# Moving two weight-update products ahead of the first mixture, and multiplying the last two down units of both mixtures unsplit

## The reference

```python
x = x + tanh(g_xattn[0]) * L0_xattn(layernorm(x), ctx, mask)   # stage 0: 16 heads of 8
x = x + tanh(g_ffn[0])   * L0_ffn(layernorm(x))                # stage 1: mixture, 16 experts, top 4
x = x + tanh(g_xattn[1]) * L1_xattn(layernorm(x), ctx, ctx)    # stage 2
x = x + tanh(g_ffn[1])   * L1_ffn(layernorm(x))                # stage 3: fake-quantised weights + LoRA
x = x + tanh(g_xattn[2]) * L2_xattn(ctx, layernorm(x))         # stage 4
x = x + tanh(g_ffn[2])   * L2_ffn(layernorm(x))                # stage 5: 8 experts, top 2
x = x + tanh(g_xattn[3]) * L3_xattn(layernorm(x), ctx, ctx)    # stage 6: 16 heads of 8
x = x + tanh(g_ffn[3])   * L3_ffn(layernorm(x))                # stage 7: mixture, 64 experts, top 6
```

```python
h = silu(einsum('th,eih->tei', x, gate_w)) * einsum('th,eih->tei', x, up_w)
routed = einsum('te,teh->th', combine, einsum('tei,ehi->teh', h, down_w))
base = einsum('bsi,oi->bso', x, fake_quant(W)) + b       # twice in L1_ffn
lora = einsum('bsr,or->bso', einsum('bsi,ri->bsr', x, A), B)   # rank 16
return base + 2 * lora
```

## Time and profile before

| | us |
|---|---|
| median of 3 runs | 596.26 |
| lowest, highest | 595.03, 597.34 |
| the profiled execution's own time | 596.09 |
| its span in the trace | 594.3 |
| busy: PE, PEld | 564.9, 409.6 |
| busy: DVE, ACT, POOL | 381.7, 387.9, 245.7 |

### The profile page before, as it was taken

How to read it: one execution, slowest core, us unless ns; L and a number is a source line. 1 busy time by engine, 2 the same in 40 slices (tenths; PEclk the granted TensorE clock), 3 DMA queues, 4 the chain that set the end, 5 groups by cost and what they waited for, 6 DMA issues and landing times.

```text
span 594.3 us, 10734 instructions
## 1 busy us (share of the span) xinstructions
PE 564.9 (95%) x3703; PEld 409.6 (69%) x3703; DVE 381.7 (64%) x736; ACT 387.9 (65%) x787; POOL 245.7 (41%) x231
## 2 busy tenths in 40 slices
PE   9999998999999997999899999999989999999997
PEld 6567766687665775776555556577768788888885
DVE  2678857556641657777354676478838666666665
ACT  4277877655666447888665656677875576666663
POOL 5006683486013100111015781000023788888884
PEclk9999999999999999999999999999999999999999
DMA  8300001161000000000000102000001666665740
GB/s 258 139 2 2 2 1 33 28 159 54 0 2 1 1 0 1 1 2 1 2 0 3 39 15 66 1 2 1 3 9 36 165 176 169 181 184 169 192 123 36
DMA packets 14852, 33.55 MB, mean 56 GB/s; under 512 B 2913, under 2 KB 8433, under 8 KB 14673
## 3 DMA queue, kind: packets, MB, share of 16 engines
q1 hardware_dynamic: 14800, 32.89, 19.4%
HBM read 32.03 MB, written 0.85 MB: 55 GB/s over the span
## 4 chain that ended last, share of the span: by engine, by line
PE 73%; DVE 9%; ACT 7%; issue 7%; POOL 3%; ACTq 0%; DVEq 0%; POOLq 0%
PE bank L842 9%; PE bank L844 8%; PE bank L843 8%; PE bank L726 5%; PE bank L737 4%; PE bank L752 3%; PE bank L685 3%; ACT wa L1408 2%; PE bank L700 2%; PE bank L648 2%; PE bank L1243 2%; PE bank L642 2%; PE bank L1118 2%; PE bank L1132 2%; PE bank L1107 1%
## 5 line engine op out<-in xcount | busy, mean ns | idle before, releaser
L502 POOL TENSOR_TENSOR h_lo<-wc,h_hi 128x512 fp32r<-128x512 f32 x56 | 72.6, 1300 | 15.2 <-ACT h_hi L1477 15.2
L842 PE MATMUL bank<-xn_hi,w_hi 128*128 128x512 f32 x168 | 66.0, 393 | 3.4 <-DVE xn_lo L1962 3.1
L844 PE MATMUL bank<-xn_hi,w_lo 128*128 128x512 f32 x168 | 65.4, 390 | 0.0
L843 PE MATMUL bank<-xn_lo,w_hi 128*128 128x512 f32 x168 | 65.4, 389 | 0.0
L1951 DVE TENSOR_TENSOR wb<-arena,bank 128x512 f32<-128x512 f32 x64 | 44.0, 687 | 32.9 <-PE bank L844 32.8
L1477 ACT ACTIVATE h_hi<-wc 128x512 fp32r<-128x512 f32 x56 | 35.3, 633 | 39.4 <-DVE wc L1959 29.8
L494 POOL TENSOR_TENSOR w_lo<-ring,w_hi 128x384 fp32r<-128x384 f32 x42 | 42.7, 1019 | 17.7 <-ACT w_hi L1454 17.7
L1739 DVE TENSOR_TENSOR wa<-bank,row_max 128x512 f32<-128x512 f32 x64 | 44.3, 692 | 7.5 <-ACT wb L1354 4.3
L1354 ACT ACTIVATE wb<-wa 128x512 f32<-128x512 f32 x64 | 40.1, 630 | 13.7 <-DVE wa L1739 13.3
L1735 DVE TENSOR_REDUCE row_max<-bank 128x4 f32<-128x512 f32 x64 | 43.6, 682 | 5.9 <-PE bank L726 5.4
L502 POOL TENSOR_TENSOR h_lo<-arena,h_hi 128x512 fp32r<-128x512 f32 x26 | 33.7, 1295 | 24.2 <-ACT h_hi L1477 24.2
(11 more groups left out here) (347 smaller groups left out, 1393.0 us busy)
## 6 DMA issues: line engine op xcount, KB each, us to landing
arena<-comb_rows SPq DMA_DIRECT2D x64, 256.0 KB, 4.1
ring<-in_experts SPq DMA_DIRECT2D x42, 192.0 KB, 2.5
ring<-in_experts SPq DMA_DIRECT2D x8, 256.0 KB, 3.2
mats<-in_mats SPq DMA_DIRECT2D x1, 1472.0 KB, 10.2
mats<-in_mats SPq DMA_DIRECT2D x1, 832.0 KB, 6.7
mats<-in_mats SPq DMA_DIRECT2D x2, 320.0 KB, 7.9
x<-in_x_t SPq DMA_DIRECT2D x1, 512.0 KB, 4.3
context<-in_ctx_t SPq DMA_DIRECT2D x1, 512.0 KB, 4.9
```

Source lines behind the costliest of these rows:

```text
L502: nc.gpsimd.tensor_tensor(h_lo[:, v % 3, :], hidden_of(v), h_hi[:, v % 3, :].bitcast(f32), ALU.subtract).then_inc(m_h_lo, 1)
L842: mm(out, w, x_, start=start, stop=False)
L843: mm(out, w, x_rest, start=False, stop=False)
L844: return mm(out, w_rest, x_, start=False, stop=stop)
```

## The change

Three things are done.

1. **The two weight updates** leave stage 1's mixture and take the place of the first two `keep_warm` calls in the drain of `attn(0)`; they write banks 3 and 2. VectorE instead of ScalarE copies them to `wd`: the first copy ahead of the last `divide`, the second behind it. The remaining idle products of the drain go to bank 1. In the mixture `combine_t` now waits for the evacuation of the values (`b_vev`) alone, and the norm's variance products wait for `d_up_out` first.
2. **The last two down products** of each mixture take the hidden activation and the ring's weights as they are, in one fp32 product each, instead of three fp32r products. The rounding on ScalarE and the rests on POOL and VectorE of these two units are gone. The counts of `m_h_hi` and `m_h_lo` are lower by two for each mixture, so the waits on them in the second subtract 2.
3. **The load of ring slot 3** for stage 5 waits until all down products of the first mixture are done, since the last pair's weights are now read from the ring itself.

```diff
@@ SP
             for e in range(4):
+                if e == 3:
+                    sp.wait_ge(m_down, MOE[0]["units"])
                 sp.dma_start(ring[:, e, 0:384], a["experts2"][e]).then_inc(w_in[e], 16)
@@ POOL, moe
-                    pool.wait_ge(m_h_hi, u0 + v + 1)
+                    pool.wait_ge(m_h_hi, u0 - 2 * n + v + 1)
...
-                for v in range(2, m["units"] - 1):
+                for v in range(2, m["units"] - 2):
                     hidden_rest(v)
@@ TensorE, attn
                 probs_v(B - 1, 3)
-                keep_warm(2, bank[3])
+                if inst == 0:
+
+                    pe.wait_ge(in_mats1, 32)
+                    mm(bank[3][:, :], lora[:, 0:P], lora[:, P:5 * P], start=True, stop=True).then_inc(d_lora, 1)
+                else:
+                    keep_warm(2, bank[3])
                 tail(B - 1, 1)
-                keep_warm(3, bank[3])
+                if inst == 0:
+                    for j in range(4):
+                        last = mm(bank[2][:, j * P:j * P + P], lora[:, 5 * P + j * P:5 * P + j * P + P],
+                                  lora[:, 9 * P:10 * P], start=True, stop=True)
+                    last.then_inc(d_lora, 1)
+                else:
+                    keep_warm(3, bank[3])
                 tail(B - 1, 2)
-                keep_warm(2, bank[3])
+                keep_warm(2, bank[1])
                 tail(B - 1, 3)
-                keep_warm(2, bank[3])
+                keep_warm(2, bank[1])
@@ TensorE, moe
                     c, slot = v % 2, slot_of(v // 2)
-                    pe.wait_ge(m_h_lo, u0 + v + 1)
+                    if v >= m["units"] - 2:
+
+                        pe.wait_ge(m_h, u0 + v + 1)
+                        mm(bank[6 + c][:, :], ring[:, slot, 256:384], hidden_of(v), start=False, stop=True)\
+                            .then_inc(m_down, 1)
+                        return
+                    pe.wait_ge(m_h_lo, u0 - 2 * n + v + 1)
...
                 for v in range(4, 6):
                     gate_up(v)
-                    if n == 0:
-                        updates1(v - 4)
                 if n == 0:
                     for half in range(2):
-                        pe.wait_ge(d_up_out, half + 1)
+                        pe.wait_ge(b_vev, half + 1)
@@ TensorE, program
             attn(0)
-            norm(NORM_OF[1][0], 2)
+            norm_means(NORM_OF[1][0])
+            keep_warm(2, bank[4])
+            pe.wait_ge(d_up_out, 2)
+            norm_rest(NORM_OF[1][0])
             moe(MOE[0])
@@ ACT, moe
-                if n == 0:
-                    for c in range(2):
-                        act.wait_ge(d_lora, c + 1)
-                        fn(wd[:, c, :], bank[2 + 3 * c][:, :], ACT.Copy).then_inc(d_up_out, 1)
...
                 for v in range(2, m["units"]):
-                    hidden(v)
+                    if v < m["units"] - 2:
+                        hidden(v)
@@ DVE, attn
                 units(base, extra)
+                if inst == 0:
+                    dve.wait_ge(d_lora, 1)
+                    v.tensor_copy(wd[:, 0, :], bank[3][:, :]).then_inc(d_up_out, 1)
                 divide(B - 1)
+                if inst == 0:
+                    dve.wait_ge(d_lora, 2)
+                    v.tensor_copy(wd[:, 1, :], bank[2][:, :]).then_inc(d_up_out, 1)
@@ DVE, moe (the same in far_gated)
                     if unit >= 3:
-                        dve.wait_ge(m_h_lo, u0 + unit - 2)
+                        dve.wait_ge(m_h_lo, u0 - 2 * n + unit - 2)
...
-                unit = m["units"] - 1
-                dve.wait_ge(m_h_hi, u0 + unit + 1)
-                dve.wait_ge(m_down, u0 + unit - 2)
-                dve.wait_ge(m_h_lo, u0 + unit)
-                v.tensor_tensor(h_lo[:, unit % 3, :], hidden_of(unit), h_hi[:, unit % 3, :].bitcast(f32),
-                                ALU.subtract).then_inc(m_h_lo, 1)
                 for c in range(2):
```

More of the change, by code:

```diff
@@ L819, in values1 @@
                     last.then_inc(b_v, 1)
[L821 to L829, removed]
             def moe(m):
@@ L864, in down @@
                     c, slot = v % 2, slot_of(v // 2)
-                    pe.wait_ge(m_h_lo, u0 + v + 1)
+                    if v >= m["units"] - 2:
[4 more added lines that the diff above has]
+                    pe.wait_ge(m_h_lo, u0 - 2 * n + v + 1)
                     product(bank[6 + c][:, :], w_hi[:, slot, 256:384], w_lo[:, slot, 256:384],
-                            h_hi[:, v % 3, :], h_lo[:, v % 3, :], v < 2, v >= m["units"] - 2).then_inc(m_down, 1)
+                            h_hi[:, v % 3, :], h_lo[:, v % 3, :], v < 2, False).then_inc(m_down, 1)
                 def weight(v):
```

## The result

The changed kernel takes 594.19 us, the median of 11 runs from 592.21 to 595.83; the kernel before, run beside it 11 times, takes 597.25 (595.03 to 599.18). The ratio is 0.9948, 95% interval 0.9935 to 0.9962: 3.1 us faster. The forecast was a gain of 4.42 and 591.8 us, and its range ended at 594.0. The prediction was wrong: the median lies 0.2 us above its range, and the gain is 1.4 us short. The profiled execution took 595.83, with a span of 594.0.

What follows compares the result with a forecast made beforehand. TensorE, at full clock and busy most of the span, was taken as the bound. -3.29 - 0.84 - 0.84 + 0.55 = -4.42 us gave 591.8 us expected, range 590.0 to 594.0.

Steps and rivals of the forecast that it cites:

- Part 1: First mixture without the two updates: the transposes of the combine weights and all behind them come earlier, -3.29 us.
- that rival: First mixture: the gain from removing the updates is not handed on, hardly any of it left, 595.1 us; chance 0.06.
- its half: First mixture: half the updates' gain kept back, 593.5 us; chance 0.15, shared with one more low-clock stretch.
- Part 2: Ends of both mixtures: unsplit last down products let the last addition start earlier, -0.84 us each.
- Part 3: Drain of the first attention: the moved updates delay transposes, reciprocal and the norm's variance products, +0.55 us.
- most of what stands there are full products: Drain of the first attention: argument, beside hardly more idle time, against the clock falling to 1.2 GHz there.
- the drain goes cold: Rival: clock falls to 1.2 GHz in the drain and stays down through norm, router and first units, 597.4 us or more; chance 0.04.
- the first rival: Low clock at other joints or nowhere: one stretch fewer, 590.4 us, chance 0.13; one more, 593.2, within a shared 0.15.

Runs made afterwards that it cites:

- changed_third: The changed kernel without an edit, one further profiled run; it kept the full clock in the drain: 591.86 us.
- down_only: The kernel before with only the last two down products of each mixture unsplit, updates left in the first mixture: 595.98 us against 597.50, ratio 0.9980.
- changed_again: The changed kernel without an edit, measured again: 593.08 us against 597.50 for the kernel before, ratio 0.9918.
- updates_only: The changed kernel with the split down products of the kernel before, so only the updates move: 594.03 us against 597.50, ratio 0.9948.
- one_for_one_16: The changed kernel with updates cut into 128x128 products of 16 rows replacing idle products one for one, both `wd` copies after the last division: 596.01 us against 596.44.
- no_idle_products: The kernel before without the first two groups of idle products in the first attention's drain: 597.39 us against 596.72, ratio 0.9989.
- the two one-for-one kernels: The changed kernel with updates as 128x128 products replacing idle products one for one: rows zero-padded to 128, 591.21 us; 16 rows, 596.01 us; both against 596.44.
- padded_rows: The changed kernel with the update products' 16-row operands zero-padded to 128 rows: 593.06 us against 596.72 for the kernel before, ratio 0.9929.
- padded_again: The changed kernel with update operands zero-padded to 128 rows, one profile more: 593.14 us.
- updates_in_gaps: The changed kernel with both updates in two TensorE pauses of the first mixture and the drain's idle products restored: 592.39 us against 597.50, ratio 0.9922.

## Why the prediction was wrong

**Part 1, -3.29: right.** -3.25 after and -3.26 in `changed_third`, with 31.70 and 31.68 us behind it where before had 31.70. All of it was handed on, so neither that rival nor its half holds.

**Part 2, twice -0.84: right.** -0.82 at the first mixture; at the end of the program the last addition ends 2.91 us behind the third last down's last record, before 3.74: -0.83. `down_only`'s five runs at the highest mean clock have a mean of 594.52 where the kernel before has 596.18: -1.66 against -1.68.

**Part 3, +0.55: the step that failed.** The waits in it were right: 1.05 us to the transposes, as taken from the mixture; the reciprocal +0.72 and the transpose +0.81 (forecast 0.8 and 0.95); POOL's slack used up; and +0.48 over the whole drain and norm where the clock holds (`changed_third`). But in the profiled run it was +1.99, 1.44 more than forecast. The forecast summed the 16-row products only by their duration, and took "most of what stands there are full products" as a reason that the clock would hold, so it put the low clock at nothing in the sum. The clock mostly didn't hold: of the profiles with 16-row products in the drain, four of five have a low stretch at 85 to 93 us (after, `changed_again`, `updates_only`, `one_for_one_16`; not `changed_third`), of the eight without them, none has. The mean clocks of all runs say the same: 4 of 42 executions with 16-row products in the drain reach 0.996, and 46 of 114 without. It is a rough sign: one of the 4 is the profiled `updates_only`, which has the low stretch. Of the two ways to explain it, fewer idle products is excluded by `no_idle_products` (4 of its 10 runs reach 0.996), and the rows are shown by the two one-for-one kernels, in profile and time. `padded_rows` and `padded_again` agree by their profiles, not by their times.

Sixteen rows alone are not enough. The same products in the mixture of the kernel before, at 108.21 and 110.85, did not lower the clock:

```profile
107.50:110.00 2.50, 2.50 (x9) 1.24 (x8) 1.09 (x5) 0.62 (x2) 0.14 (x1) 1.00 0.00 0
110.00:112.50 2.50, 2.00 (x12) 1.36 (x11) 0.00 (x0) 1.54 (x3) 0.00 (x0) 1.00 0.00 0
```

Nor did those of `updates_in_gaps` at 96.04 and 102.32. What the drain has besides that makes them matter there is not shown by any run.

**The rivals.** The mechanism that happened stood there as "the drain goes cold", at 0.04, but priced as all or nothing from four stretches on; what came was a single stretch, worth 1.4 to 1.5 us (14.46 and 14.53 against 13.02). Only `one_for_one_16` shows the long form that the rival describes. Forecast plus one such stretch is 593.2, a value that the first rival had, for another joint; that it had a chance there is luck.

**From 593.2 to 594.19.** The kernel before gave 596.26 in the three runs that the forecast started from and 597.25 in the eleven beside the changed one. Its time goes with the mean granted clock: over the 63 runs beside the experiments, by class and as means, 596.18 at 0.996 or more (24 runs), 597.12 around 0.994 (17), 598.76 around 0.991 (21). The changed kernel's 18 runs: 591.86 at 0.996 or more (3), 592.55 around 0.994 (4), 594.2 around 0.991 (10); one run of each lies lower still. At equal mean clock, a comparison that leaves the price of the low clock out, the change gains 4.3 to 4.6, as forecast (4.42). The first measurement gained 3.1: none of its eleven runs is in the highest class (3 of all 18), against 24 of 63 before. The low drain is worth as much as the missing 1.4, but `changed_again` gained 4.4 with the low drain in its profile, so how much of the 1.4 is the drain and how much chance stays open. The other low stretches (10 to 15, 152 to 157, 167 to 178, 292 to 305, 440 to 447 and the last 7 us) come in some executions and not in others, in the kernel before too; no run here says why.

The Trainium skill, TensorE: Matmul & The Clock Gate, section "HAM oscillation — how this bites in real kernels", names idle gaps between bursts of matmuls, in its example long waits for DMA, as what puts the engine back to half its rate. The rows of this drain show another cause. The changed kernel has no idle time ahead of the fall (5.00 of 5 us busy, then 0.50), and `no_idle_products`, with pauses of 0.51 and 0.68 us, keeps 1.00 at 4.07 of 5. The prediction took the earlier trace rows, 4.03 of 5 us busy ahead of a low stretch, as agreement with that section; a drain just as busy and at full clock takes that away. In this joint the rows counted, not the gaps.

## What to carry to other kernels

Work that takes the place of idle products has two prices, its duration and what it does to the clock. If it uses few of the array's rows, try it padded with zero rows (a 128x512 product took 1.12 us either way) and in the size and place of what it replaces; here that made the two updates free. Compare a kernel's terms between profiles at the same granted clock, by distances between two events of one stretch, before you call a forecast's term wrong. An unsplit fp32 product paid at the end of an accumulation, where rounding and rest are a chain over three engines, even though it costs TensorE 0.86 us and its three split records 0.66.

## What was unexpected of the hardware

Products of 16 rows are recorded as busy for as long as full ones (1.12 us for 128x512 either way), yet in the drain TensorE fell to 1.2 GHz behind them in four of five profiles, once in all windows from 87.5 to 102.5; the same products with zeros in the other 112 rows left it at 2.4 GHz in three of three. The transposes behind the padded product came 0.97 us after its start, behind the 16-row one 1.05; the weight load's idle time between them went from 0.76 to 0.28 us. With 128 rows the first load of the transposes began at 84.91, 0.58 us behind the product's start and while it ran; with 16 rows it began at 85.79, 1.05 behind (`changed_third`, product at 84.74).
